# The attention stage of a fused cross-attention and expert layer, fed with x and weights that also come in turned

## What is computed

```
xn = layernorm(x)
q = xn @ Wq.T + bq;  k = ctx @ Wk.T + bk;  v = ctx @ Wv.T + bv
x = x + softmax(q @ k.T) @ v
# 8 experts, each takes the 256 tokens per batch with the largest probability
p = softmax(layernorm(x) @ gate_w); top_p, top_idx = top_k(p.T, 256)
y = gelu(layernorm(x)[top_idx] @ w1[e]) @ w2[e] * top_p
out = x, with y added at top_idx
```

## Time and profile before

| | us |
|---|---|
| median of three runs | 521.34 (520.19 to 521.48) |
| the profiled execution | 523.48 |
| its span, first to last instruction | 521.7 |
| start of the last residual (group 7) | 69.83 |
| variances complete, last of the attention stage | 73.91 |
| first expert's first matmul | 129.68 |

### The profile page before, as it was taken

How to read it: one execution, slowest core, us unless ns; L and a number is a source line. 1 busy time by engine, 2 the same in 40 slices (tenths; PEclk the granted TensorE clock), 3 DMA queues, 4 the chain that set the end, 5 groups by cost and what they waited for, 6 DMA issues and landing times.

```text
span 521.7 us, 9685 instructions
## 1 busy us (share of the span) xinstructions
PE 467.1 (90%) x3208; PEld 415.5 (80%) x3208; DVE 304.7 (58%) x827; ACT 222.0 (43%) x549; POOL 202.9 (39%) x167
## 2 busy tenths in 40 slices
PE   4999936545999999999999999999999999999990
PEld 4787724435899989998988999899998988989890
DVE  3568658886745655655575466557555664654430
ACT  1368859500325524542544355245424533543320
POOL 4354330006028134640834282355408243822404
PEclk9989985555999999999999999999999999999995
DMA  7912325202505072424427151724434271412213
GB/s 225 338 53 94 110 80 215 118 1 75 172 16 88 22 201 46 78 84 117 71 52 193 29 82 24 198 52 72 111 90 73 50 201 31 82 22 31 24 18 40
DMA packets 34098, 47.98 MB, mean 92 GB/s; under 512 B 3745, under 2 KB 29474, under 8 KB 33570
## 3 DMA queue, kind: packets, MB, share of 16 engines
q0 software_dynamic: 12288, 17.08, 18.7%
q1 hardware_dynamic: 21794, 30.71, 17.8%
HBM read 30.72 MB, written 16.92 MB: 91 GB/s over the span
## 4 chain that ended last, share of the span: by engine, by line
PE 78%; DVE 8%; ACT 5%; issue 2%; DMA 2%; SPq 2%; POOL 1%; ACTq 0%; DVEq 0%; POOLq 0%
PE wide L798 35%; PE bank L784 34%; PE bank L623 4%; DMA x_all<-in_x_dram 2%; ACT ysb L519 2%; DVE over L962 2%; ACT prb L525 2%; DVE floor L975 1%; POOL out_dram L447 1%; PE wide L623 1%; PE bank L759 1%; DVE cand L957 1%; PE bank L700 1%; DVE reached L969 1%; PE wide L730 1%
## 5 line engine op out<-in xcount | busy, mean ns | idle before, releaser
L447 POOL DMA_INDIRECT out_dram<-ysb,sidx x64 | 105.0, 1641 | 112.4 <-ACT ysb L584 95.6
L798 PE MATMUL wide<-w2hi,hhi 128*128 128x256 f32 x512 | 147.8, 289 | 0.0
L798 PE MATMUL wide<-w2hi,hlo 128*128 128x256 f32 x512 | 144.9, 283 | 0.0
L798 PE MATMUL wide<-w2lo,hhi 128*128 128x256 f32 x512 | 144.5, 282 | 0.0
L574 ACT ACTIVATE hraw<-bank 128x512 f32<-128x512 f32 x128 | 76.3, 596 | 136.3 <-PE bank L784 136.3
L439 POOL DMA_INDIRECT xg<-xn_rows,gidx x64 | 65.1, 1017 | 158.6 <-issue 89.4
L1118 DVE CAST hhi<-hraw 128x512 fp32r<-128x512 f32 x128 | 55.0, 430 | 96.9 <-ACT hraw L574 96.9
L798 PEld LDWEIGHTS wide<-w2hi,hhi 128*128 128x128 f32 x512 | 96.9, 189 | 4.0
L798 PEld LDWEIGHTS wide<-w2lo,hhi 128*128 128x128 f32 x512 | 96.6, 189 | 3.7
L798 PEld LDWEIGHTS wide<-w2hi,hlo 128*128 128x128 f32 x512 | 96.5, 189 | 0.0
L1120 DVE TENSOR_TENSOR hlo<-hraw,hhi 128x512 fp32r<-128x512 f32 x128 | 88.8, 694 | 4.4
(11 more groups left out here) (149 smaller groups left out, 496.8 us busy)
## 6 DMA issues: line engine op xcount, KB each, us to landing
w1raw<-in_L_ffn_w_dram SPq DMA_DIRECT2D x8, 1024.0 KB, 5.9
w2raw<-in_L_ffn_w_dram SPq DMA_DIRECT2D x8, 1024.0 KB, 10.0
xn_rows<-x_all SPq DMA_DIRECT2D x4, 1060.0 KB, 4.0
out_dram<-x_all SPq DMA_DIRECT2D x8, 512.0 KB, 2.9
x_all<-in_x_dram SPq DMA_DIRECT2D x3, 1024.0 KB, 10.6
x_all<-in_x_dram SPq DMA_DIRECT2D x2, 512.0 KB, 6.0
xg<-xn_rows,gidx POOLq DMA_INDIRECT x64, 2.8
out_dram<-ysb,sidx POOLq DMA_INDIRECT x64, 4.0
```

What stands on the lines that cost most here:

```text
L447: pool.indirect_dma_start(out=out_rows, out_offset=at, in_=ysb[g][:, i, :], in_offset=None, compute_op=ALU.add).then_inc(rows_added, 16)
L798: t = pe.matmul(o, hh[s % 4][:, i * P:(i + 1) * P], w[:, j, :], start=(j == 0 and m == 0 and i % 2 == 0), stop=(j == HC - 1 and m == 2), s ...
```

## The change

- **Inputs.** The host also gives x turned (`x_turned`, 256 x 4 x 1024), and gives the context and Wk turned in place of as they are; Wv comes both ways. The small vectors and the gate weights come as one array `small`. ACT issues five of the loads, SP the others.
- **Fold.** PE turns neither the context nor Wk nor Wv. DVE subtracts from Wq the mean of each of its rows. So the scores can be made from raw x, and neither `xc` nor `xcT` exists any more.
- **Steps.** A group's scores are made one step earlier (j = g+1), from the loaded tile of turned x in `raw`, a ring of four. They alternate between two banks; `score`, `nmax` and `prb` have two buffers each. `raw` is also the place of `w1raw` and `w2raw`, whose first load waits for the last scores. Turned x of groups 4 to 7 is loaded when the ring is free.
- **Sums.** The values get a column of ones, so PE also forms the sum of the exponentials; ACT takes no sums in L525's place; DVE inverts that column out of PSUM at the head of the residual.
- **Order.** On DVE the scores come before `bn_stats`; the copy of the extra columns moves to ACT; `nm2` is gone, its sign goes into the square's scale. POOL keeps only the power.
- **Filler.** In steps 2 to 7 PE turns the identity six times between scores and values.
- All twelve steps are written out, with no loop.

```diff
-            sp.dma_start(wk_sb[:], Wk.rearrange("(k p) d -> p k d", p=P)).then_inc(kv_loaded, 16)
-            sp.dma_start(ctx_sb[:], ctx_in.rearrange("b s d -> (b s) d").rearrange("(k p) d -> p k d", p=P)).then_inc(kv_loaded, 16)
...
-            for b in range(1, B):
-                sp.dma_start(x_all[:, b, :, 0:C], x_v[b]).then_inc(x_rest, 16)
...
+            sp.dma_start(wkT[:], WkT.rearrange("(k p) d -> p k d", p=P)).then_inc(kv_loaded, 16)
             sp.dma_start(wq_sb[:], Wq.rearrange("(k p) d -> p k d", p=P)).then_inc(q_loaded, 16)
...
+            def load_turned(g):
+                sp.dma_start(raw[:, g % 4], xT_g[:, :, g // GB, g % GB * GP:(g % GB + 1) * GP]).then_inc(xT_loaded[g], 16)
+
+            for g in range(NG):
+                if g < 4:
+                    load_turned(g)
+                sp.dma_start(xcols(g), x_g[:, g // GB, g % GB]).then_inc(x_loaded[g], 16)
...
             def step(j):
+                if active(j, 1) and j - 1 + 4 < NG:
+                    sp.wait_ge(scored, j)
+                    load_turned(j - 1 + 4)
...
+            def first_weights():
+                sp.wait_ge(scored, NG)
+                sp.dma_start(w1raw[:], w1[0].rearrange("(k p) h -> p k h", p=P)).then_inc(raw_loaded, 16)
+                sp.dma_start(w2raw[:], w2[0].rearrange("(k p) d -> p k d", p=P)).then_inc(raw_loaded, 16)
...
@@ ScalarE
+            act.dma_start(ctxT[:], ctxT_in.rearrange("(k p) s -> p k s", p=P)).then_inc(kv_loaded, 16)
+            act.dma_start(small_sb[:], small).then_inc(small_loaded, 16)
+            act.dma_start(wvT[:, :, 0:C], WvT.rearrange("(k p) d -> p k d", p=P)).then_inc(v_loaded, 16)
+            act.dma_start(wv_sb[:], Wv.rearrange("(k p) d -> p k d", p=P)).then_inc(v_loaded, 16)
+            act.dma_start(bv_ext[:, 0:C], bv.rearrange("(a d) -> a d", a=1)).then_inc(v_loaded, 16)
...
-                    act.wait_ge(extra_ready, g + 1)
-                    m, ss = columns_of(nm2, g), columns_of(ss2, g)
+                    m, ss = extra_cols(g)[:, :, E:EX], columns_of(ss2, g)
                     for i in range(GT):
                         act.wait_ge(x1_ready, GT * g + i + 1)
-                        act.activation(sq[:, i, :], xcols(g)[:, i, :], ACT.Square, bias=m[:, i:i + 1],
+                        act.activation(sq[:, i, :], xcols(g)[:, i, :], ACT.Square, bias=m[:, i, :], scale=-1.0,
                                        accum_out=ss[:, i:i + 1]).then_inc(squared, 1)
...
                     act.wait_ge(max_ready, g + 1)
+                    wait_count(act, prb_turned, g - 1)
                     for i in range(GT):
-                        a = act.activation(prb[:, i, :], score[:, i, :], ACT.Exp, bias=nmax[:, i:i + 1],
-                                           accum_out=psums[:, i:i + 1])
+                        a = act.activation(prb[g % 2][:, i, :], score[g % 2][:, i, :], ACT.Exp, bias=nmax[g % 2][:, i:i + 1])
...
@@ TensorE
+                    pe.wait_ge(xT_loaded[g], 16)
+                    if g == 0:
+                        pe.wait_ge(qk_ready, 1)
+                    wait_count(pe, score_ready, g - 1)
+                    wait_count(pe, extra_ready, g - 1)
+                    for i in range(GT):
+                        for k in range(KC):
+                            t = pe.matmul(score_bank(g)[:, i], raw[:, g % 4, k, i * P:(i + 1) * P], qk[:, k, g // GB, :],
+                                          start=(k == 0), stop=(k == KC - 1))
+                    t.then_inc(scored, 1)
+                if 1 < j < NG:
+                    keep_warm(bank[2], 6)
...
@@ VectorE
+            dve.wait_ge(q_loaded, 16)
+            dve.tensor_reduce(wq_mean[:], wq_sb[:], AX.X, ALU.add).then_inc(wq_summed, 1)
+            dve.wait_ge(wq_summed, 1)
+            dve.tensor_scalar(wq_mean[:], wq_mean[:], 1.0 / C, None, ALU.mult).then_inc(wq_summed, 1)
+            dve.wait_ge(wq_summed, 2)
+            for k in range(KC):
+                dve.tensor_scalar(wq_sb[:, k], wq_sb[:, k], wq_mean[:, k:k + 1], None, ALU.subtract).then_inc(wq_ready, 1)
...
+                    dve.wait_ge(attended, g + 1)
+                    dve.reciprocal(rinv[:].unsqueeze(2), wide[:, :, CX:VX]).then_inc(rinv_ready, 1)
```

More of the change, by code:

```diff
@@ L43, in wait_count, with build @@
     eng.wait_ge(sem, n)
-def build(nc, x, ctx_in, Wq, bq, Wk, bk, Wv, bv, gate_w, w1, w2, out):
+def build(nc, x, xT, ctxT_in, Wq, WkT, Wv, WvT, bv, small, w1, w2, out):
     B, T, C = x.shape
-    S = ctx_in.shape[1]
+    S = ctxT_in.shape[1] // B
     E, _, H = w1.shape
@@ L75, in build @@
     CX = C + EX
+    VX = CX + 1
+    GP = GT * P
     assert UB == HB and NU == 2
@@ L195, in build @@
         v_loaded = sem("v_loaded")
-        x_first = sem("x_first")
-        x_second = sem("x_second")
-        x_rest = sem("x_rest")
+        small_loaded = sem("small_loaded")
+        x_loaded = [sem(f"x_loaded{g}") for g in range(NG)]
+        xT_loaded = [sem(f"xT_loaded{g}") for g in range(NG)]
+        wq_summed = sem("wq_summed")
+        wq_ready = sem("wq_ready")
         consts = sem("consts")
@@ L289, in build @@
         LAST = 4
-        N_CONST = 13
+        N_CONST = 15
         def active(j, stage):
-            return not isinstance(j, int) or 0 <= j - stage < NG
+            return 0 <= j - stage < NG
         def run_steps(eng, body, after={}):
-            for j in range(LAST + 1):
+            for j in range(NG + LAST):
                 body(j)
@@ L301, in run_steps, with score_bank @@
                     after[j]()
-            with eng.Fori(LAST + 1, NG) as j:
-                body(j)
-            for j in range(NG, NG + LAST):
-                body(j)
-                if j in after:
-                    after[j]()
+        def score_bank(g):
+            return bank[g % 2][:, 0:GT * SX].rearrange("p (i s) -> p i s", i=GT)
         def counts(h):
@@ L691, in step @@
             def step(j):
[L692 to L702 removed]
                 if active(j, 3):
                     g = j - 3
[L705 removed]
+                    if g == NG - 1:
                         keep_warm(bank[0], 8)
@@ L729, in step @@
                     for i in range(GT):
-                        t = pe.matmul(wide[:, i, 0:CX], prbT[:, i * P:(i + 1) * P],
-                                      v_sb[:, bass.ds(g // GB, 1), :], start=True, stop=True)
+                        t = pe.matmul(wide[:, i, 0:VX], prbT[:, i * P:(i + 1) * P], v_sb[:, g // GB, :], start=True, stop=True)
                     t.then_inc(attended, 1)
-            run_steps(pe, step, {1: folded_keys, 2: values, 4: odd_values})
+            run_steps(pe, step, {0: folded_keys, 1: values, 4: odd_values})
             with pe.Fori(0, 2 * ROUNDS) as r:
```

250 lines of the change are left out of this document (98 added, 152 removed).

## The result

| | before | after | predicted |
|---|---|---|---|
| median, runs of one session | 521.41 (4 runs, 520.19 to 521.99) | 513.76 (4 runs, 513.08 to 514.52) | 511.5 |
| ratio, with its 95% interval | | 0.9853 [0.9838, 0.9868] | 0.981 |
| the profiled execution | 523.48 | 514.52 | 513.7 |
| first residual | 31.56 | 26.20 | 27.4 |
| last residual (group 7) | 69.83 | 63.30 | 61.5 |

The change brings 7.65 us of the 9.8 forecast.

A forecast was written before the change was run, and what follows sets the result against it. Only the stage up to the variances changes, bound by its start (PE's work, waiting for x) and a PE-ACT loop in the steps. Start -4.1, steps -4.4, end -1.25 sum to -9.75, taken as 9.8: 521.34 becomes 511.5 us, range 509 to 514.5.

The forecast's parts named there:

- three signs of being wrong: PE waiting for a load in steps 3 to 6, PE's clock below 1.00 after 30 us, or changed time after the variances.
- The start: Up to the first residual: earlier PE start and dropped turns bring it from 31.5 to 27.4, -4.1 us (bounds -5.3, -1.5).
- the 1.8 us for the slow clock and the gate step: Before group 0's scores: added for PE's later full speed, centring Wq and a gate step awaiting loads; 12.4 becomes 14.2.
- the loads are in time: Start and step 5: x covered by 2 us, the odd values' move landing at 31.6, needed at 32.4.
- The steps: First to last residual: 33.9 us against 38.3, -4.4 (bounds -5.8, -1.5), by a chain over DVE and PE's work.
- E(3) to E(8): From PE's end of values in step 3 (27.4) to step 8 (53.45); two steps take at least 10.85 us.
- the line on the last two steps, E(8) to E(10): PE's end of values, step 8 to step 10: 53.45 to 61.3, where the last two steps had taken 10.15 us.
- The 3.36 from turn to next residual: Last step: time from PE's turn of group 7's exponentials to the last residual, read before the change (66.47 to 69.83).
- Rival C: PE's clock falls to 1.2 GHz inside the steps, making the kernel slower, 538 us from step 4 to 9; chance 0.05.
- The end: Last residual to variances: reciprocal first and squares following each residual, 2.85 us against 4.1, -1.25 (bounds -1.5, -0.7).
- Behind the variances: After the last variances: the same instructions follow, so no change, with the same 55.8 us to the experts' first matmul.
- Written out: Steps: dropping the loop's register work, which goes for three steps, was counted at nothing.

The follow-up runs named there:

- the second run: The changed kernel measured once more with no edit: median 515.24 us (4 runs), ratio 0.9862 to the kernel before; its profiled execution took 515.45.
- ACT's issue: Against the version with all edits: ACT, not SP, issues the DMA moving the odd values, behind ACT's copies; 536.51 us, ratio 1.0269 to the kernel before.
- the version with all edits: Changed kernel plus seven early PE matmuls, maxima before statistics, fillers only in steps 4 to 7, twelve in step 9, more before the experts: 509.46 us, ratio 0.9751.
- the start matmuls: Changed kernel plus seven matmuls of a constant tile on PE while it waits for the first loads: 513.70 us, ratio 0.9829 to the kernel before.

## Why the prediction was right, and where it was not

**The total.** 7.65 us for 9.8; the median of 513.76 lies in the forecast's own range of 509 to 514.5. That it came so near is partly luck: in the profiled execution the steps fell short by 3.2 us, and a start 1.3 and a time behind the variances 1.1 us better than forecast made up for most of that. Of the three signs of being wrong that the forecast had named, two came: PE's clock was below 1.00 after 30 us, and the time after the variances changed.

**The start** gave -5.4 for -4.1 in the profiled execution, and -2.7 in the second run. PE began at 4.74, not 4.2; the scores of group 0 came at 12.95, not 14.2. The mis-sized term is the 1.8 us for the slow clock and the gate step: only the keys' matmuls ran slowly in the profiled execution, so that the term should have been next to nothing (12.4 plus the 0.5 by which PE began later gives 12.9), and in the second run the fold did too, so that the scores came 2.7 us later than in the first. The term is not one number. The step that the loads are in time held: the move of the odd values, issued at 20.66, landed 9.1 us later (29.8), 1 us ahead of its use. So did the judgement that PE's fold, not only x, sets the start: loading x by groups alone moved the first residual by 1.85 us of the 5.4.

**The steps** are the step that failed. Up to group 5 all is as forecast: two steps take 10.6 us (4.94 + 5.66) where 10.85 stood, alternating as drawn, and E(3) to E(8) is 25.6 us for 26.05. What failed is the line on the last two steps, E(8) to E(10): 7.85 forecast, 8.8 with the clock held (second run), 11.5 in the profiled execution. Two things were missing. First, an edge that I had not listed: the values of a group overwrite `wide`, and so wait for the last group's residual. In the steps of the middle the scores cover that, ahead of the turn before the change and between turn and values after it; in step 9 there are none left, and PE idles 1.4 us. So PE comes to its last turn at 59.17 in the second run, 0.7 us after the exponentials' end (58.49), where 0.1 is enough elsewhere. The 3.36 from turn to next residual, taken from the earlier trace rows, became 4.04 in the second run (59.17 to 63.21): 0.4 are the same edge in step 10, the rest the reciprocal at the head of the residual, counted in the other steps and left out here. Second, what followed from the pause: the clock fell, and the step that takes 4.57 in the second run (54.44 to 59.01) took 6.43, the one behind it 5.08 instead of 4.20. So of the 3.2 us that the whole term is short, 2.7 are the clock and 0.5 the rest (the wait, less what the steps up to group 5 did better).

**Rival C** was named with the right price. I gave it 0.05, thinking of the pause of every second step; in the changed kernel it came in step 9, from another pause, and took two steps. Three of my own variants then had it for most of the steps: without the fillers, with ACT's sums, with ACT's issue. So 0.05 was too low for a kernel this near to it. That the fillers hold the clock is shown by the run without them. That they count as work is not shown by that run, since it also doubles the pause; it is shown by the rises among transposes alone, in the earlier trace rows and from 57.44 to 60.24 in the changed kernel. These speak against the Trainium skill's sentence that the full clock doesn't engage for transposes (TensorE: Matmul & The Clock Gate, Part 4: PE-mode transpose).

**The end** gave -1.4 for -1.25.

**Behind the variances** I had 0 and it was -1.1. The instructions are the same, but the clock stood at another point of its rise: the same fillers and turned rows took 3.81 + 1.09 here, 4.50 + 1.49 in the second run and 4.50 + 1.61 before. "The same instructions, so the same time" was wrong by 1.1 us in one execution and by 0.1 in the other.

**Written out** I had counted at nothing; on the kernel before it is 0.6 us in the steps and 0.2% of the time (about 1.15 us) in all.

What stays open: why the clock fell after a pause of 1.41 us in one execution and not after one of 1.42 in the next. The length of the pause alone does not decide. The clock fell after pauses of 0.80 us (kernel before, at 26 us) and 0.68 (written out, at 24 us), and held after one of 0.94 in the version with all edits; and behind the last values, with PE idle, it stayed up for at least 1.4 us in that version, 3.0 in the changed kernel and 3.2 in the kernel before. Open too are why the residual of group 6 starts 0.67 us after its reciprocal in the changed kernel (57.55 to 58.22), elsewhere 0.29; and where the slower executions of the kernel with fillers in step 9 lost their 2 us.

## What to carry to other kernels

When a step loses work on PE, look for each wait that this work covered, the overwriting of a buffer included, and ask whether PE now pauses: near such a pause the price can be not its microsecond but the clock, here up to 27 us. Filler that costs 0.7 us a step and looks useless in the sum can be what holds a kernel together, and a kernel whose executions spread over several microseconds may be one whose clock is decided by chance (compare the mean granted clocks, and the first matmuls' durations); close its pauses first, and judge other edits only then. A DMA moved to a busy engine's queue is a piece of work on that engine, at the place where it stands.

## What the runs showed of the hardware

- At 1.2 GHz PE did not recover by being busy: without a pause it was busy for 30 us without the fillers (33 to 63), for 37 with ACT's sums (32.2 to 69.7) and for 57 with ACT's issue (21.1 to 78.6). It did come back while or right after PE ran filler transposes (57.44 to 60.24 in the changed kernel, 76.02 to 78.67 with ACT's issue, and ahead of the experts in the earlier trace rows). Rows of only six fillers (1.48 us at this clock) between scores and values did not bring it back, in four steps with ACT's issue and three with ACT's sums. That the longer rows bring it back is a coincidence seen each time, not tested by itself.
- The granted clock reads 1.00 for the start, though matmuls there take twice their later time (2.08 us for four that took 1.13 behind the start matmuls). Read the duration of a matmul of a known shape there, not the clock.
- A small DMA waits behind the loads issued ahead of it: 133 KB landed 9.1 and 10.2 us after issue on SP's queue, where loads were still pending, and 6.5 on ACT's. In the kernel before, issued on SP's queue at 27.12 with no load pending, it landed after 2.7.
- The one DMA issue in the middle of ACT's work took 0.70 us of its time; the five at the start of the changed kernel took 0.47 to 0.77 each.
